# An accumulating transfer in place of a selector matmul: the global attention row in a fused attention and expert kernel

## The reference, cut to what matters

```python
h = _layernorm(x) * (1 + ca) + sa
...
local = jnp.einsum('bnst,bnte->bnse', attn, V)
...
global_out = jnp.einsum('bnm,bme->bne', attn_g, Vg)
out = local + global_out[:, :, None, :]
...
x = x + ga * (out @ Wo.T + bo)
h = _layernorm(x) * (1 + cb) + sb
x = x + gb * _ffn(h)     # router, top 1 of 16 experts, 512 places each
```

## Time and profile before

| | |
|---|---|
| median of three runs | 1859.71 us (1859.41 to 1863.76) |
| the profiled execution's own time | 1857.97 us |
| its span, first to last instruction | 1856.3 us |
| PE busy | 1812.6 us, 98% of the span |
| PEld busy | 1494.7 us, 81% |
| DVE busy | 1169.2 us, 63% |
| ACT busy | 832.3 us, 45% |
| POOL busy | 797.9 us, 43% |
| mean granted clock | 0.992 |

### The profile page before, as it was taken

One profiled execution on the slowest core, in us unless ns is written; L12 is line 12 of the kernel. 1 busy time (PEld: TensorE's weight loads), 2 busy tenths in 40 slices (PEclk: granted clock), 3 DMA queues, 4 the chain that ended last, 5 costly groups with the idle time before them and its releaser, 6 DMA issues.

```text
span 1856.3 us, 28238 instructions
## 1 busy us (share of the span) xinstructions
PE 1812.6 (98%) x9177; PEld 1494.7 (81%) x9194; DVE 1169.2 (63%) x1880; ACT 832.3 (45%) x1329; POOL 797.9 (43%) x665
## 2 busy tenths in 40 slices
PE   8999999999999899999999999998998999999998
PEld 3688888888887468888888888887887888888886
DVE  4577788788787654556645454548648796455862
ACT  2544554654654433334433333345446464334542
POOL 2134445545453421424434142426547766233642
PEclk9999999999999899999999999999999999999999
DMA  8344654654664544344443434345454655435622
GB/s 283 137 142 123 196 137 117 196 140 114 193 190 142 134 144 147 133 147 140 165 153 130 169 127 157 124 143 186 150 188 166 211 189 184 144 119 169 216 82 68
DMA packets 146379, 287.56 MB, mean 155 GB/s; under 512 B 17905, under 2 KB 18493, under 8 KB 146326
## 3 DMA queue, kind: packets, MB, share of 16 engines
q1 hardware_dynamic: 115354, 221.27, 34.0%
q0 software_dynamic: 30976, 65.64, 14.0%
HBM read 237.71 MB, written 67.49 MB: 164 GB/s over the span
## 4 chain that ended last, share of the span: by engine, by line
PE 93%; DVE 3%; issue 2%; ACT 1%; DMA 1%; POOL 0%; POOLq 0%; DVEq 0%; another core or an unknown queue 0%; ACTq 0%; SPq 0%
PE bank L333 27%; PE bank L335 27%; PE bank L334 27%; PE bank L733 3%; PE bank L604 1%; PE bank L813 1%; PE bank L895 1%; PE bank L725 1%; PE bank L542 1%; PE bank L593 1%; PE bank L713 1%; PE bank L703 0%; DVE h_lo L1623 0%; PE bank L740 0%; PE bank L708 0%
## 5 line engine op out<-in xcount | busy, mean ns | idle before, releaser
L1623 DVE TENSOR_TENSOR h_lo<-h_f,h_hi 128x512 fp32r<-128x512 f32 x256 | 219.6, 879 | 358.2 <-ACT h_f L1222 358.0
L1221 ACT ACTIVATE h_hi<-bank,b_col 128x512 fp32r<-128x512 f32 x256 | 176.4, 689 | 596.7 <-PE bank L335 582.6
L333 PE MATMUL bank<-bt_hi,w_hi 128*128 128x512 f32 (+4 forms) x1024 | 361.2, 353 | 6.9 <-DVE w_lo L1596 4.5
L335 PE MATMUL bank<-bt_hi,w_lo 128*128 128x512 f32 (+4 forms) x1024 | 359.4, 351 | 0.0
L334 PE MATMUL bank<-bt_lo,w_hi 128*128 128x512 f32 (+4 forms) x1024 | 359.4, 351 | 0.0
L333 PE MATMUL bank<-w_hi,h_hi 128*128 128x512 f32 x832 | 325.8, 392 | 1.6 <-issue 1.6
L334 PE MATMUL bank<-w_lo,h_hi 128*128 128x512 f32 x832 | 324.2, 390 | 0.7 <-issue 0.7
L335 PE MATMUL bank<-w_hi,h_lo 128*128 128x512 f32 x832 | 324.1, 390 | 0.0
L333 PEld LDWEIGHTS bank<-bt_hi,w_hi 128*128 128x128 f32 x1024 | 194.6, 190 | 33.3 <-issue 9.5
L334 PEld LDWEIGHTS bank<-bt_lo,w_hi 128*128 128x128 f32 x1024 | 194.8, 190 | 21.2 <-issue 0.2
L335 PEld LDWEIGHTS bank<-bt_hi,w_lo 128*128 128x128 f32 x1024 | 194.6, 190 | 20.3
(11 more groups left out here) (283 smaller groups left out, 3163.7 us busy)
## 6 DMA issues: line engine op xcount, KB each, us to landing
raw<-in_L_ffn_W_dram SPq DMA_DIRECT2D x128, 1024.0 KB, 5.5
xa<-in_L_attn_x_dram SPq DMA_DIRECT2D x16, 1024.0 KB, 5.3
xr<-in_L_attn_x_dram SPq DMA_DIRECT2D x16, 1024.0 KB, 8.3
h_rows<-sb_tab SPq DMA_DIRECT2D x16, 1024.0 KB, 10.2
out_dram<-xr SPq DMA_DIRECT2D x16, 1024.0 KB, 12.2
h_rows<-h POOLq DMA_DIRECT2D x16, 1024.0 KB, 9.5
b_bc<-in_L_ffn_b_dram SPq DMA_DIRECT2D x16, 256.0 KB, 6.3
wm_a<-in_L_wmod_dram SPq DMA_DIRECT2D x2, 1024.0 KB, 10.8
```

The source lines that it names most:

```text
L333: pe.matmul(o, a_hi, b_hi, start=start, stop=False)
L335: return pe.matmul(o, a_lo, b_hi, start=False, stop=stop)
L1221: act.activation(h1_hi[b % 2][:, j, :], h_bank[j][:, :], ACT.Relu, bias=bias)
L1623: dve.tensor_tensor(h1_lo[b % 2][:, j, :], h1_f[:, j, :], h1_hi[b % 2][:, j, :].bitcast(F32), ALU.subtract) \
```

## The change

The global row leaves PE. In the prologue the 64 global rows are multiplied by their batch's gate `ga`, in float32, and stored in DRAM as 64 rows. To have the gate in 64 rows, a small matmul (GAROW, a 4x64 selector by the 4 gate rows), a copy by ACT and one product by DVE are new; four DVE operations that split the rows into three bf16 parts go, and so do two DVE memsets, and POOL makes a 4x64 selector in place of a 128x512 one.

In each turn POOL issues an accumulating transfer that adds the four gated rows of group i, each repeated for 128 tokens, to `xr` of group i (`add_global`, after `scatter` and ahead of the inverse root). DVE's `residual` of that group, one turn later, waits for it in place of the load. The four bf16 matmuls of a turn and the load of `grows` go.

SP loads `xr` and stores the shift rows at the head of the turn, and after them waits for the last query row and loads `xa`. On DVE `route_slots` and `probs_low` come ahead of the three query rows, in this order.

```diff
-    global_dram = nc.dram_tensor("global_rows", (NSEG * 3, D), BF16, kind="Internal").ap()
+    global_dram = nc.dram_tensor("global_rows", (NSEG, D), F32, kind="Internal").ap()
...
@@ sync
-        sp.wait_ge(g_split_done, 1)
-        sp.dma_start(global_dram.rearrange("(n t) d -> n t d", t=3), g_split[:]).then_inc(g_stored, 16)
+        sp.wait_ge(g_gated, 1)
+        sp.dma_start(global_dram, g_ga[:]).then_inc(g_stored, 16)
...
-            if load2:
-                sp.wait_ge(t1_full, 4 * i.n + 4)
-                sp.wait_ge(qc_raw, 4 * i.n + 4)
-                load_x(i.plus(2))
             if cur:
-                wait_past(sp, av_full, 4 * i.n - 4)
-                sp.dma_start(grows[i.par][0:3 * GS, :], global_dram[bass.ds(i.n * 3 * GS, 3 * GS), :]) \
-                    .then_inc(grows_in[i.par], 16)
                 if not isinstance(i.n, int) or i.n >= 2:
                     sp.wait_ge(xn2_done, 4 * i.n - 4)
                     stand_alone(sp, sp_passed)
...
                 sp.dma_start(group_rows(h2_dram, i), shift).then_inc(shift_stored[i.par], 16)
+            if load2:
+                sp.wait_ge(t1_full, 4 * i.n + 4)
+                sp.wait_ge(qc_raw, 4 * i.n + 4)
+                load_x(i.plus(2))
@@ tensor
+        pe.wait_ge(mod_fixed, 2)
+        pe.wait_ge(made, POOL_MADE)
+        bank_free(GAROW)
+        product(GAROW, pe.matmul(pro_bank(GAROW)[0:NSEG, :], seg_batch[:], modr[:, GA, :], start=True, stop=True))
...
-            split3(pe, big[s][:, :], pt_hi[:, s, :], pt_lo[:, s, :], u_hi[:, s, :], u_lo[:, s, :], True, False)
-            pe.matmul(big[s][:, :], seg_sel[:, s, :], grows[g.par][:], start=False, stop=True).then_inc(av_full, 1)
+            split3(pe, big[s][:, :], pt_hi[:, s, :], pt_lo[:, s, :], u_hi[:, s, :], u_lo[:, s, :], True, True) \
+                .then_inc(av_full, 1)
...
-                pe.wait_ge(grows_in[p1.par], 16 * (p1.half + 1))
@@ scalar
+        copy_out(GAROW, g_b[:], pro_bank(GAROW)[0:NSEG, :])
@@ vector
-        dve.tensor_copy(g_split[:, 0, :], g_a[:]).then_inc(gsum_step, 1)
...
-        dve.tensor_tensor(g_split[:, 2, :], g_x[:], g_split[:, 1, :], ALU.subtract).then_inc(g_split_done, 1)
+        dve.tensor_tensor(g_ga[:], g_a[:], g_b[:], ALU.mult).then_inc(g_gated, 1)
...
-        dve.wait_ge(g_split_done, 1)
...
             if nxt:
                 stats1(i.plus(1))
+            if prev3:
+                route_slots(p3)
+            if prev:
+                probs_low(p1)
             if cur:
                 for s in range(GS if last_turn else GS - 1):
                     query_row(i, s)
...
             if prev:
-                probs_low(p1)
-            if prev3:
-                route_slots(p3)
-            if prev:
...
-                dve.wait_ge(xr_in[p1.par], 16 * (p1.half + 1))
+                dve.wait_ge(xr_summed[p1.par], 16 * (p1.half + 1))
@@ gpsimd
+        def add_global(g):
+            pool.wait_ge(xr_in[g.par], 16 * (g.half + 1))
+            stand_alone(pool, pool_passed)
+            part = global_dram[bass.ds(g.n * GS, GS), :].unsqueeze(0).to_broadcast([P, GS, D])
+            pool.dma_start(xr[g.par][:], part, accum_op=ALU.add).then_inc(xr_summed[g.par], 16)
...
             if prev3:
                 scatter(i.plus(-3))
+            if isinstance(i.n, int) and i.n == 0:
+                pool.wait_ge(g_stored, 16)
+            add_global(i)
             if prev:
                 inverse_root(p1.n, ln2_ready, ln2_rstd, VE2, MN2, RS2, NR2)
```

More of the change, by code:

```diff
@@ L123, in build_block @@
     ones = keep("ones", [P, P], BF16)
-    seg_sel = keep("seg_sel", [P, GS, P], BF16)
-    grows = [keep(f"grows{i}", [P, D], BF16) for i in range(2)]
+    seg_batch = keep("seg_batch", [NBATCH, NSEG], F32)
     QUAD = P // KC
@@ L201, in build_block @@
                                       ("bqk", [NBATCH, 2, D], F32), ("hg_t", [P, KC, NSEG], F32))
-    g_split, brow, u_row, gg_t = over(r_tab + 8 * KB, ("g_split", [NSEG, 3, D], BF16), ("brow", [P, D], F32),
+    g_ga, brow, u_row, gg_t = over(r_tab + 8 * KB, ("g_ga", [NSEG, D], F32), ("brow", [P, D], F32),
                                       ("u_row", [1, D], F32), ("gg_t", [P, KC, NSEG], F32))
@@ L264, in build_block @@
     gsum_masked, gsum_negb, gsum_exp, gsum_prob = (sem(f"gsum_{k}") for k in ("masked", "negb", "exp", "prob"))
-    g_split_done, g_stored, table_cleared = sem("g_split_done"), sem("g_stored"), sem("table_cleared")
+    g_gated, g_stored, table_cleared = (sem(k) for k in ("g_gated", "g_stored", "table_cleared"))
     x_in = [sem(f"x_in{i}") for i in range(2)]
     xr_in = [sem(f"xr_in{i}") for i in range(2)]
-    grows_in = [sem(f"grows_in{i}") for i in range(2)]
+    xr_summed = [sem(f"xr_summed{i}") for i in range(2)]
     ln1_step, ln1_ready, ln1_rstd, xn_done = (sem(k) for k in ("ln1_step", "ln1_ready", "ln1_rstd", "xn_done"))
@@ L335, in split3 @@
         return pe.matmul(o, a_lo, b_hi, start=False, stop=stop)
-    (MCH, SCT, BCOL, FIRST4, WOT, UCOL, MCOL, VCH, HGT, LATE4, GROWS, GGT, SG, BROW, SCOL, PGT, TG,
-     B1T, PRO_END) = (0, 4, 5, 6, 7, 11, 12, 13, 17, 18, 19, 20, 21, 22, 23, 24, 25, 26, 27)
+    (MCH, SCT, BCOL, FIRST4, WOT, UCOL, MCOL, VCH, HGT, LATE4, GROWS, GGT, SG, BROW, SCOL, PGT,
+     GAROW, TG, B1T, PRO_END) = (0, 4, 5, 6, 7, 11, 12, 13, 17, 18, 19, 20, 21, 22, 23, 24, 25, 26, 27, 28)
     def pro_bank(q):
@@ L352, in build_block @@
     POOL_MADE = 9
-    DVE_MADE = 9
+    DVE_MADE = 7
     def results_done(eng, e, b):
@@ L759, in last_turns @@
             pe.wait_ge(pt_split, Z.n + 1)
-            pe.wait_ge(grows_in[Z.par], 16 * (Z.half + 1))
             for s in range(GS):
@@ L1265, in _ @@
         dve.memset(count[:], 0.0).then_inc(init_made, 1)
-        dve.memset(grows[0][:], 0.0).then_inc(init_made, 1)
-        dve.memset(grows[1][:], 0.0).then_inc(init_made, 1)
         dve.memset(pg[:], 0.0).then_inc(init_made, 1)
@@ L1530, in last_turns @@
             dve.wait_ge(h2_stored[Z.par], 16 * Z.half)
-            dve.wait_ge(xr_in[Z.par], 16 * (Z.half + 1))
+            dve.wait_ge(xr_summed[Z.par], 16 * (Z.half + 1))
             residual(Z, 0)
@@ L1724, in _ @@
         pool.memset(ones[:], 1.0).then_inc(made, 1)
-        pool.memset(seg_sel[:], 1.0).then_inc(made, 1)
+        pool.memset(seg_batch[:], 1.0).then_inc(made, 1)
         pool.wait_ge(made, 3)
@@ L1729, in _ @@
                            channel_multiplier=-1).then_inc(made, 1)
-        pool.affine_select(out=seg_sel[:], in_=seg_sel[:], compare_op=ALU.is_ge, fill=0.0, base=0,
-                           pattern=[[-3, GS], [0, P]], channel_multiplier=1).then_inc(made, 1)
+        spb = NSEG // NBATCH
+        pool.affine_select(out=seg_batch[:], in_=seg_batch[:], compare_op=ALU.is_ge, fill=0.0, base=0,
+                           pattern=[[1, NSEG]], channel_multiplier=-spb).then_inc(made, 1)
         pool.wait_ge(made, 5)
-        pool.affine_select(out=seg_sel[:], in_=seg_sel[:], compare_op=ALU.is_ge, fill=0.0, base=2,
-                           pattern=[[3, GS], [0, P]], channel_multiplier=-1).then_inc(made, 1)
+        pool.affine_select(out=seg_batch[:], in_=seg_batch[:], compare_op=ALU.is_ge, fill=0.0, base=spb - 1,
+                           pattern=[[-1, NSEG]], channel_multiplier=spb).then_inc(made, 1)
         pool.iota(tokids[:], pattern=[[P, NSEG]], base=0, channel_multiplier=1).then_inc(made, 1)
```

## The result

The changed kernel takes 1847.66 us (median of six runs, 1843.6 to 1849.87), the kernel before 1860.82 beside it (1859.3 to 1863.76). The medians differ by 13.2 us (a quotient of 0.9929); the ratio on record is 0.9921, with a 95% interval of 0.9911 to 0.9931. The forecast was 13.9 us less, or 1845.8, in a range of 1842.5 to 1856. The profiled execution took 1845.40 us, its span is 1843.8; before these were 1857.97 and 1856.3, so the two traces differ by 12.5 us of span. The traced execution of the kernel before is a quick one: all that were timed beside the changed kernel and its variants took 1858.47 us or more. So a difference of medians can come out larger than the same difference of traces.

The account below looks back on a forecast made before the run. The prediction took PE's list of matmuls to bound the turn. Its terms, -14.6 (PE), +0.8 (DVE stalls), -0.4 (prologue) and +0.3 (first group), sum to -13.9 us, or 1845.8 us, range 1842.5 to 1856.

Parts of the forecast that it names:

- What is removed from PE: PE's `attend`: dropping four bf16 matmuls saves 0.96 us a turn, 14.6 us in all, at most 15.4.
- The sum: All terms over the whole kernel: -14.6 + 0.8 - 0.4 + 0.3 = -13.9 us, giving 1845.8 us.
- The third rival: PE's `attend`: the bf16 matmuls' 0.24 us is a restart needed anyway, so 1858 to 1860 us; chance 0.05.
- The new order on DVE: DVE in each turn: slots and `probs_low` ahead of the query rows fit; 0.8 us charged in all for stalls.
- The first margin: DVE in a steady turn: `probs_low` ends 0.8 us before PE's `attend` wants its result.
- the second: DVE in a steady turn: the residual's first product empties its bank 0.6 us before PE wants it.
- POOL and the transfers: POOL and DMA in each turn: the 1.43 us issue is hidden in 2.2 us of idle time, the transfers too.
- the bound above: POOL's issue of `add_global`: at most four times 1.43 = 5.7 us, if the repeated rows go in smaller pieces.
- The rival's mechanism: POOL's list becomes the chain: a late `xr` or long issue holds the inverse root and scores; about 1871 us, chance 0.07.
- Prologue: Start of the kernel: the new matmul's 0.7 us disappears in PE's idle time and 0.4 us is gained.
- First group: Group 0's `xr` load and sum, wanted by the residual at about 104 us: 0.3 us lost, bounds 0 to 6.
- Fifteen turns without a loss: Turns 1 to 15: `attend` lies where PE never waits, so 15 x 0.96 = 14.4 us is gained.

Follow-up runs that it names:

- the narrow matmul: The kernel before with the bf16 matmul of `attend` cut to 128 of its 512 columns: 1851.05 us, ratio 0.9943.
- The four issues: The changed kernel with the accumulating transfer of a turn issued as four of one segment each: 1846.34 us, ratio 0.992.
- the second trace of the changed kernel: The changed kernel, unaltered, run again beside the version with DVE's old order in the last turn alone: 1847.33 us, ratio 0.9929.

## Why the prediction was right, and where its terms were off

**What is removed from PE: right.** The step of 0.96 us a turn measured 0.97 in the timeline of PE and 0.99 in the pitch. The sum counts 61 bf16 matmuls on the path. Sixty of them lie in three stretches of the table, which give 1.08 + 12.90 + 0.99 = 14.97 us; the one left, the first segment of the last turn's `attend`, lies in that turn's 9.80 and was lost there. The third rival (no effect) is ruled out by the pitch with and without the bf16 matmuls. How the 0.24 us divides into columns and restart is not settled: the narrow matmul shows only that it is neither alone.

**The new order on DVE: the stall was put in the wrong place, and the order's worth was missed.** The prediction kept the slots' stalls at their median and charged 0.8 us. The slots ran unstalled, and the query rows, which now lie beside `normalise1`, took 0.46 us more each, twice a turn. The first margin was so larger than forecast (1.1 us for 0.8), the second smaller (0.2 for 0.6, and 0.05 to the weight load), and both held. The Trainium skill's rule (SBUF — State Buffer, "Who interferes with whom": an exclusive lock on the shared pair) agrees in kind, as the stretched operations read two SBUF operands while POOL works on SBUF; it names the right partner, and the order of the list, not the median of before, says which instruction meets it. Not every such meeting was costly: the slots' small operations of two SBUF operands took their usual 0.16 us beside POOL's power. What the prediction did not see at all is that the old order would have cost 0.2 us a turn as soon as the bf16 matmuls were gone: it compared the new order with the slack of before, not with the old order in a shorter turn.

**POOL and the transfers: right in the steady turns.** Issue 1.06 us for 1.43; the root released by DVE; PE kept waiting by no sum. Only "the `xa` load keeps its wait and its time" is wrong, as the next but one paragraph shows. The four issues took 3.73 us where the bound above was 5.7, and in the steady turns even these were hidden. The rival's mechanism is real: with the `xr` load late by SP's old order the time is 164 us above the changed kernel's.

**Prologue: right in sign from the new matmul on.** -0.63 us for -0.4, and PE's idle time is gone. What lies ahead of the new matmul is below.

**First group: the sum was late as foreseen, and `xa` too; 0.7 us for 0.3.** In the new order of SP the third group's `xa` load stands behind the shift store, and was issued at 89.75 us where it was at 83.30; DVE's statistics of the second turn waited 1.21 us for it. That comes from SP's order and not from the transfer: in the run without the transfer the wait is 1.19 us, and there PE lost next to nothing by it (10.89 us to the first L813, where the kernel before has 10.78 and the changed kernel 11.47). The rest is the transfer's. The first sum was issued at 93.69 us and landed 11.6 us later, at 105.29, and the first residual started at 105.36, 0.11 us later than without the transfer. Its addition then lay beside an operation of `normalise1` and took 1.17 us for 0.70, while in the run without the transfer `normalise1` took the longer, 4.81 us for 4.23. The 0.6 us runs on through the statistics, POOL's root and ACT to `u_lo`, for which PE's scores waited 0.42. In the second trace of the changed kernel the first residual stood idle 0.63 us up to the landing of the sum, and PE waited 0.41 for it. The version with DVE's old order takes 10.79 us to the first L813, but it lost more a stretch earlier, where PE waited 1.47 us ahead of `attend` (32.06 us to the third group's rows, for 30.30):

```profile
105.94 0.47 PE L332 MATMUL bank<-u_hi,pt_hi 128*128 128x512 f32 x1 [1.47 <-issue]
```

**Fifteen turns without a loss: mis-sized in the last turn.** `attend` of the last turn was counted as a turn like the others. Its order change turned 0.24 us of gain into 0.67 of loss, as the experiment with the old order there shows; 0.9 us could be had back.

**The early 1.6 us: open.** The stretch from 30 to 40 us was granted 0.69 of the clock in the profiled run, and 0.83 before. The version with four issues, whose prologue is the same, was granted 0.83 and reached the mark of 72.80 at 71.50, and so the new prologue need not cost the 1.6 us. But that is the rarer case. Of the eight traces with the new prologue, two were granted 0.83 (marks at 71.08 and 71.50) and six 0.66 to 0.69 (72.80 to 73.42); the three with the old one were all granted 0.83 (71.18 to 71.34). Whether the change makes the lower clock likelier is not shown, and no run tried the prologue's edits by themselves. The windows of the kernel before and of the version with four issues:

```profile
30.00:40.00 10.00, 10.00 (x26) 4.61 (x27) 1.12 (x2) 1.39 (x3) 0.00 (x0) 0.83 0.77 284
...
30.00:40.00 10.00, 9.76 (x26) 4.58 (x27) 1.30 (x3) 1.17 (x4) 0.00 (x0) 0.83 0.81 297
```

The sum has no term for it. Without the 1.62 the traces give -12.5 - 1.62 = -14.1 us, close to the -13.9 of the sum, and partly by luck: 0.8 of stalls that did not come, 0.6 more from the steady turns and 0.2 more in the prologue stand against 0.4 more in the second turn, 0.9 in the last one and 0.1 behind it.

## What to carry to other kernels

When PE's list is the turn, work taken off it pays in full only as long as every engine that feeds it still fits into the shorter turn: compute the old order's slack in the new turn, and see whether a reorder is needed rather than merely harmless. Check each reorder again in the turns that stand alone, since what filled the time in front of a wait in a steady turn may be missing there. A wait put into an in-order queue (here POOL's for `xr`) must have its producer moved up with it, in the same edit.

## What the runs showed of the hardware

A bf16 matmul of 128 columns between split float32 ones cost 0.14 us, one of 512 columns 0.24. A DVE product of two 128x512 operands from SBUF beside POOL's `normalise1` took 1.15 us in place of 0.69, twice in the turn shown, while operations of 128x4 and 128x12 beside POOL's power took their usual 0.16 to 0.17. In the second turn, where two versions differ by 0.11 us in the start of the residual, DVE's addition took 1.17 us for 0.70 in one, and POOL's `normalise1` beside it 4.81 for 4.23 in the other. The granted clock of one program differed between runs at the same place (0.50 and 1.00 behind the last turn, 0.69 and 0.83 in a shared prologue), and such a difference went with 1.3 to 1.8 us, more than the smaller effects studied here.
